# A decoder layer on one core: a new stage order in the attention groups, and FFN preparation moved into the last of them

## What is computed

```python
x = x + attn_ref(layernorm(x), ...)          # one head, softmax over channels
x = x + xattn_ref(layernorm(x), ctx, ...)    # context-query attention
x = x + ffn_ref(layernorm(x), ...)           # mixture of 8 experts and a shared one
# xattn_ref, c = layernorm(x), q = ctx:
s = (c @ w_c + b_c)[:, :, None] + (q @ w_q + b_q)[:, None, :] + cq
a = softmax(s, axis=2);  c2q = a @ q
b_att = softmax(max(s, axis=2), axis=1);  q2c = b_att @ c
z = concat([c, c2q, c * c2q, c * q2c]) @ W_l.T + b_l
# ffn_ref: sigmoid routing picks 4 of 8 experts by groups, weights cw
y = sum_e cw[e] * (silu(x @ Wg[e]) * (x @ Wu[e])) @ Wd[e] + shared(x)
```

## Time and profile before

| | us |
|---|---|
| runs of the kernel | 728.39, 731.85, 733.77 |
| median | 731.85 |
| time of the profiled execution | 728.91 |
| its span, first to last instruction | 726.7 |
| eight attention groups, to the first transposes of the second block | 440.3 |
| FFN block from there | 286.4 |
| PE busy in the span | 674.6 |

### The profile page before, as it was taken

How to read it: one execution, slowest core, us unless ns; L and a number is a source line. 1 busy time by engine, 2 the same in 40 slices (tenths; PEclk the granted TensorE clock), 3 DMA queues, 4 the chain that set the end, 5 groups by cost and what they waited for, 6 DMA issues and landing times. The chain is left out here.

```text
span 726.7 us, 11807 instructions
## 1 busy us (share of the span) xinstructions
PE 674.6 (93%) x3880; PEld 568.7 (78%) x3880; DVE 488.8 (67%) x1253; ACT 346.7 (48%) x793; POOL 243.0 (33%) x321
## 2 busy tenths in 40 slices
PE   3998989999999999999968887999999999999997
PEld 2867968878788788787857576888888888888886
DVE  5577686776776767867675886766666667676432
ACT  3644755565457455664545625433342523433331
POOL 2134364153252542542540412332322232232222
PEclk9999999999999999999997998999999999999999
DMA  7605034042051250430531009131323223030300
GB/s 209 165 25 169 5 83 138 0 135 85 25 157 37 61 159 0 127 93 25 162 102 29 26 15 321 45 129 56 117 88 116 87 98 104 4 143 30 118 29 30
DMA packets 51773, 64.43 MB, mean 89 GB/s; under 512 B 3912, under 2 KB 49528, under 8 KB 50848
## 3 DMA queue, kind: packets, MB, share of 16 engines
q1 hardware_dynamic: 51744, 64.06, 29.0%
HBM read 56.60 MB, written 7.45 MB: 88 GB/s over the span
## 5 line engine op out<-in xcount | busy, mean ns | idle before, releaser
L1515 POOL TENSOR_TENSOR sg<-sg,cw_wide 128x512 f32<-128x512 f32 x56 | 74.6, 1333 | 178.0 <-ACT sg L1476 176.1
L1480 ACT ACTIVATE a_hi<-af 128x512 fp32r<-128x512 f32 x63 | 39.8, 632 | 144.5 <-DVE af L1537 144.5
L1537 DVE TENSOR_TENSOR af<-bank,sg 128x512 f32<-128x512 f32 x63 | 43.3, 687 | 61.6 <-POOL sg L1515 57.1
L75 PE MATMUL bank<-h_hi,w_lo 128*128 128x512 f32 x168 | 67.4, 401 | 1.6 <-DVE w_lo L1554 0.8
L1542 DVE TENSOR_TENSOR a_lo<-af,a_hi 128x512 fp32r<-128x512 f32 x63 | 47.2, 749 | 31.4 <-ACT a_hi L1480 31.4
L76 PE MATMUL bank<-h_lo,w_hi 128*128 128x512 f32 x168 | 66.1, 394 | 0.0
L77 PE MATMUL bank<-h_hi,w_hi 128*128 128x512 f32 x168 | 66.0, 393 | 0.0
L948 POOL TENSOR_TENSOR wz_lo<-tmp,wz_hi 128x512 fp32r<-128x512 f32 x28 | 36.4, 1310 | 44.7 <-ACT wz_hi L732 44.7
L582 PE MATMUL bank<-ctxtf,ctw 128*112 128x375 f32 x128 | 47.0, 489 | 3.0 <-DVE ctw L1089 3.0
L75 PE MATMUL bank<-wl_hi,op_lo 128*112 128x256 f32 x128 | 39.9, 312 | 9.3 <-DVE op_lo L1073 9.3
L75 PE MATMUL bank<-w_hi,a_lo 128*128 128x256 f32 x168 | 47.4, 282 | 0.0
(11 more groups left out here) (229 smaller groups left out, 2059.4 us busy)
## 6 DMA issues: line engine op xcount, KB each, us to landing
ctxtf<-in_ctx_t SPq DMA_DIRECT2D x32, 375.0 KB
ctxf<-in_ctx SPq DMA_DIRECT2D x32, 375.0 KB
cw_wide<-cw_scratch SPq DMA_DIRECT2D x7, 1536.0 KB, 8.0
xt<-in_x SPq DMA_DIRECT2D x8, 448.0 KB, 9.6
x_scratch<-x2b SPq DMA_DIRECT2D x8, 448.0 KB, 3.3
x2n<-x_scratch SPq DMA_DIRECT2D x7, 512.0 KB, 4.6
cw_wide<-cw_scratch SPq DMA_DIRECT2D x7, 512.0 KB, 4.6
x2t<-x_scratch SPq DMA_DIRECT2D x7, 512.0 KB, 3.9
```

The costliest lines, as they stand in the source:

```text
L75: pe.matmul(dst, a_lo, b_hi, start=first, stop=False, **kw)
L1480: act.activation(a_hi[n % (AHEAD + 1)][:, :], af[(p + n) % 2][:, :], ACT.Copy).then_inc(a_hi_ok, 1)
L1515: pool.tensor_tensor(sg[b][:, :], sg[b][:, :], cw_wide[p][:, ORDER[n], :], ALU.mult).then_inc(sgw_ok, 1)
L1537: dve.tensor_tensor(af[b][:, :], u_bank[b][:, :], sg[b][:, :], ALU.mult).then_inc(af_ok, 1)
```

## The change

What it does, engine by engine:

- **All groups, PE.** Stream 3's `z_c` is split into two halves that are put behind `attention_out(3)` and behind `turn_c(2)`; `probs_proj(3)`, `attention_out(1)` and others move a little; `turn_x(3)` and `z_c2q(1)` go ahead of the wait for `mrow`.
- **All groups, ACT and DVE.** `c_weighted` of streams 0 and 1 moves from DVE to ACT (an Identity with scale and bias). On DVE `x1_moments(3)` goes ahead of `sim_max(0)`, and `x2_sum(i - 1, 1)` goes from there to behind `sim_max(2)`. Two one-column copies are added.
- **All groups, POOL.** `c_lo`, and with it `x2b`, waits until `normalise_h` of the next group is done.
- **Front of group 7.** `load_norm(sp, 0)` goes ahead of the nine weight loads. `normalise3(0)` goes behind `probs_low(1)`; `turn_h3(0)` behind `probs_proj(1)`; the shared expert's split on ACT behind `h3_high`; expert 0's and 1's splits to before `ct_copy(0)`; the gate's split to group 0.
- **Rest of group 7.** The second FFN group's `moments3`, `rstd3`, `normalise3` and `turn_h3`, the silu, product and split of the shared expert, the silu input of expert 0 (`sg[1]`) and `gate_up_early` of expert 1 come in. Experts 2 to 5 are loaded into the context's memory as `c2q_product` frees it, and the routing weights are spread to all partitions there. These are taken out of the second block.

The core of the diff:

```diff
                     if last:
+                        for j in range(STAGED):
+                            sp.wait_ge(c2q_mm, G * i + j + 1)
+                            for half, w in enumerate((wg, wu)):
+                                sp.dma_start(gate_up_weights(w_staged[j])[:, half, :, :],
+                                             w[DONE + j].rearrange("(k p) n -> p k n", p=P)).then_inc(wx_in[DONE + j], 16)
+                            sp.dma_start(w_staged[j][:, GU:GU + D], wd[DONE + j]).then_inc(wx_in[DONE + j], 16)
                         sp.wait_ge(cwt_ok, 1)
                         sp.wait_ge(w_in, 16)
                         sp.dma_start(cw_dram[0], cwt[:, :]).then_inc(cw_st, 16)
+                        sp.wait_ge(cw_st, 16)
+                        sp.dma_start(cw_wide0[:, 0:EARLY, :], cw_dram[0][0:EARLY, :].partition_broadcast(P)).then_inc(cw_in, 16)
+                        sp.dma_start(cw_wide0[:, EARLY:NEXP, :], cw_dram[0][EARLY:NEXP, :].partition_broadcast(P)).then_inc(cw_rest_in, 16)
...
+                sp.wait_ge(x2_st, 16 * 3)
+                load_norm(sp, 0)
...
-                sp.wait_ge(x2_st, 16 * 3)
-                load_norm(sp, 0)
                 group(NGRP - 1, True)
...
+                    probs_proj(0)
+                    probs_proj(1)
                     if last_group:
                         pe.wait_ge(v_ok, KB * (i + 1))
                         turn_h3(pe, 0)
-                    probs_proj(0)
-                    probs_proj(1)
                     probs_proj(2)
                     attention_out(0)
+                    probs_proj(3)
+                    attention_out(1)
                     if last_group:
                         pe.wait_ge(gate_ok, 1)
                         logits(pe, 0, h3_hi0, h3_lo0, h_bank[1])
-                    probs_proj(3)
-                    attention_out(1)
                     attention_out(2)
+                    if not is_first(i):
+                        z_c(i - 1, 2)
+                    turn_c(0)
+                    attention_out(3)
                     if last_group:
                         pe.wait_ge(lgt_ok, 1)
                         turn_logits(pe, 0)
                     if not is_first(i):
-                        z_c(i - 1, 2)
-                    turn_c(0)
-                    if not is_first(i):
-                        z_c(i - 1, 3)
-                    attention_out(3)
+                        z_c_half(i - 1, 3, 0)
                     turn_c(1)
                     similarity(0)
                     turn_c(2)
+                    if not is_first(i):
+                        z_c_half(i - 1, 3, 1)
                     similarity(1)
                     turn_c(3)
                     similarity(2)
...
+                    turn_x(3)
+                    z_c2q(1)
                     pe.wait_ge(mrow_ok, i + 1)
-                    turn_x(3)
                     for j in range(G):
                         last = pe.matmul(m_bank[:, j * L:(j + 1) * L], ident[0:G, j:j + 1].to_broadcast([G, P]), mrow[:, :],
                                          start=True, stop=True)
                     last.then_inc(b_mm, 1)
-                    z_c2q(1)
                     z_x3(0)
                     z_c2q(2)
                     z_x3(1)
@@ -706,8 +737,14 @@
                         turn_cw(pe, 0, h_bank[1])
                         pe.wait_ge(w01_lo_ok, 1)
                         gate_up_early(1, wqkv_hi[:, 0, :], wqkv_lo[:, 0, :])
+                        pe.wait_ge(cwt_ok, 1)
+                        pe.wait_ge(cb_ok, i + 1)
+                        turn_h3(pe, 1)
                         for j in range(G):
                             z_c(i, j)
+                        pe.wait_ge(af_ok, 1)
+                        pe.wait_ge(w01_lo_ok, 2)
+                        gate_up_early(0, wqkv_hi[:, 1, :], wqkv_lo[:, 1, :])
...
+                    if last:
+                        h3_high(act, 0, h3_hi0)
+                        act.wait_ge(shared_in, 48)
+                        act.activation(shared_hi[:, 0:GU + D], shared_f[:, :], ACT.Copy).then_inc(shared_hi_ok, 1)
                     probs_proj_copy(2)
                     if last:
+                        act.wait_ge(w01_in, 96)
+                        act.activation(wqkv_hi[:, 0, :], w_f01[:, 0, :], ACT.Copy).then_inc(w01_hi_ok, 1)
+                    probs_proj_copy(3)
+                    if last:
                         copy_logits(act, 0, h_bank[1])
-                    probs_proj_copy(3)
+                        act.activation(wqkv_hi[:, 1, :], w_f01[:, 1, :], ACT.Copy).then_inc(w01_hi_ok, 1)
                     ct_copy(0)
+                    c_weighted(0)
                     ct_copy(1)
+                    c_weighted(1)
...
                     if last:
+                        act.activation(silu_warm[:, :], mhalf2[:, 0:1], ACT.Silu)
+                        act.wait_ge(gu_mm, 1)
+                        act.activation(sg[0][:, :], bank[0][:, :], ACT.Silu).then_inc(sg_ok, 1)
+                        act.wait_ge(af_ok, 1)
+                        act.activation(op_hi0[:, :], af[0][:, :], ACT.Copy).then_inc(a_hi_ok, 1)
+                        copy_cw(act, 0, h_bank[1])
+                        act.wait_ge(gu_mm, 3)
+                        act.activation(sg[1][:, :], bank[1][:, :], ACT.Silu).then_inc(sg_ok, 1)
                         for j in range(G):
                             wz_high(i, j)
-                        copy_cw(act, 0, h_bank[1])
                     else:
                         residual(i + 1)
                         h_high_pair(i + 1, 1)
...
+                    if last:
+                        w01_low(0)
                     for j in range(G):
                         rstd2(j)
-                    if not last:
+                    if last:
+                        rstd3(pool, 1)
+                        w01_low(1)
+                        pool.wait_ge(h3_ok, 2 * T)
+                    else:
                         ln1_scalars(i + 1)
-                    if last:
-                        for e in range(2):
-                            pool.wait_ge(w01_hi_ok, e + 1)
-                            pool.tensor_tensor(wqkv_lo[:, e, :], w_f01[:, e, :], f32(wqkv_hi[:, e, :]), ALU.subtract).then_inc(w01_lo_ok, 1)
+                        pool.wait_ge(hh_ok, G * (i + 2))
                     pool.wait_ge(c_hi_ok, i + 1)
                     pool.tensor_tensor(c_lo[:, :, :, :], ct[:, :, :, :], f32(c_hi[:, :, :, :]), ALU.subtract).then_inc(c_lo_ok, 1)
...
                     c_rows(1)
-                    if last:
-                        dve.wait_ge(wk_in, 48)
-                        sum_logits(dve, 0)
                     dve.wait_ge(st2_ok, ev[2])
-                    c_weighted(0)
+                    dve.tensor_copy(held[0:L, 0:1], mhalf[:, 0:1])
                     x1_moments(2)
                     x1_sum(3)
                     x1_stats(3)
                     c_rows(2)
-                    c_weighted(1)
+                    if last:
+                        dve.wait_ge(wk_in, 48)
+                        sum_logits(dve, 0)
                     dve.wait_ge(st2_ok, ev[3])
+                    dve.tensor_copy(held[0:L, 0:1], mhalf[:, 0:1])
+                    x1_moments(3)
                     sim_max(0)
-                    x1_moments(3)
-                    if not is_first(i):
-                        x2_sum(i - 1, 1)
                     c_rows(3)
                     c_weighted(2)
...
                     for n in range(1, NE):
                         expert(g, p, n)
 
-                with pool.Fori(0, NG2 // 2) as it:
-                    group(2 * it, 0, False)
+                group(0, 0, False)
+                with pool.Fori(0, NG2 // 2 - 1) as it:
                     group(2 * it + 1, 1, False)
+                    group(2 * it + 2, 0, False)
+                group(NG2 - 2, 1, False)
                 group(NG2 - 1, 0, True)
 
             @block.vector
@@ -1554,20 +1616,24 @@
```

154 lines of the change are left out of this document (90 added, 64 removed).

## The result

| | kernel before | changed kernel |
|---|---|---|
| time, median (lowest to highest) | 730.61 us (728.39 to 733.77, 4 runs) | 706.22 us (703.79 to 707.51, 4 runs) |
| ratio to before | | 0.9674, 95% interval 0.9645 to 0.9704 |
| span of the profiled execution | 726.7 us | 703.7 us |

What follows compares the result with a forecast made beforehand. PE, busy 93% of the span, was taken to bound the kernel. 9.0 + 3.5 + 10.5 + 3.5 - 1.0 = 25.5 us saved gives 703.4 us profiled, 706 from the median; 8-in-10 range 697 to 714 us.

Steps and rivals of the forecast that it cites:

- A: Similarity section, all eight groups: PE's stops for c and ctw go, 1.13 us a group, 9.0 us saved.
- B: x_low wait, groups 0 to 6: 1.2 us removed comes back waiting for xt; only clock loss is saved, 3.5 us.
- Rival 4: Similarity section: c still comes from POOL's rstd, the stops stay, A is lost; 715 us, chance 0.04.
- Rival 2: Load of xt doesn't limit; B gives 1.2 us in six more groups; 699 us, chance 0.11.
- The clock recovery: Half-clock losses hidden by the wait for xt go: 2.5 us after group 0, 1.0 after group 2, together 3.5.
- Rival 1: Clock falls at the new stop before probs_proj(0), 1.7 us each, over five groups 8.5; 714 us, chance 0.13.
- C: Front of group 7: x2n lands earlier, first sum comes at 381.7 instead of 392.69; 10.5 us saved.
- D: End of group 7 across the barrier: fourth gate product at 444.6 instead of 448.09; 3.5 us saved, 1.0 lost to clock.
- Rival 5: POOL's held-back work slows x3_low; 1.6 us in each of seven groups reaches PE, 11.5; 717 us, chance 0.04.
- Rival 3: Group 7's new ACT and POOL splits land on the path, taking back C and D's gains; 711 us, chance 0.08.
- Rival 6: Slower: x2_sum(1) slips past c2q_product(0), delaying context loads and xt; at 7 us late, 736 us; chance 0.02.

Runs made afterwards that it cites:

- experiment 2: split_context with c_weighted(0) and (1) back on DVE, 694.61 us; with z_c(3) whole ahead of attention_out(3), 688.71 us; base 686.85 us.
- experiment 1: Changed kernel without POOL's wait for normalise_h, 705.51 us; with context loads split, 686.85; with both edits, 701.12; the split alone on the kernel before, 722.33.
- no_hold: Changed kernel without POOL's wait for normalise_h ahead of c_lo; 705.51 us, ratio 0.9683 to the kernel before.
- norm3_early: split_context with normalise3(0) back ahead of inv_sum(0) in group 7; 688.50 us against the base's 686.85 us.
- experiment 4: Changed kernel with expert 1's gate and up products back behind the barrier, 703.45 us; with split context loads too, 686.57; POOL's expert 1 split also moved, 685.58.
- split_third_w01: Changed kernel with split context loads, expert 1's gate and up products behind the barrier, POOL's low split of expert 1 behind the x2b sums; 685.58 us.
- split_context: Changed kernel with each 125-partition context load cut into 112 and 13 partitions; 686.85 us, ratio 0.9425 to the kernel before.

## Why the prediction was right, and where it wasn't

**The total** was right, 706 forecast and 706.2 measured; 25.5 us were to go, and 24.4 went by the medians (23.0 by the spans). Two terms were off in opposite ways, A 1.4 more than its 9.0 and B 4.1 less than its 3.5, so part of how close the total came is luck.

**A** held. No wait for `ctw` is left, two for `c` are (0.7 us, in group 0), and 8.21 us pass from `turn_c(0)` to `c2q_product(0)` (8.4 forecast). The term was mis-sized by 0.18 us a group; experiment 2 shows that a stop costs two to three times its row. Rival 4 is out.

**B's mechanism** held, and this was the forecast's boldest step: a wait is removed that is the largest sum among PE's in the groups, and nothing is won, since `xt` lands no earlier. `normalise_h` takes 1.37 us (near 1.5), PE waits instead before `probs_proj(0)`, and DVE waits for `xt` by the trace. The four cells of experiment 1 show it as cause, not only as reading. Rival 2 is out: with it the hold would have been worth its price without the split. The clock recovery, "together 3.5", came: after group 0 the gap is 35.15, was 37.80, 2.65 won where 2.5 stood, and after group 2 it is 0.6 shorter, where 1.0 stood. The step that failed is that nothing else moves in B: that `xt` comes as before and that the clock stays up behind the new stop. In group 1 the gap is 39.78, was 36.26, 3.5 us that the sum put at nothing. Rival 1 happened there, once instead of five times: a stop of 3.48 us before `probs_proj(0)`, and 6.8 us at 1.2 GHz behind it. In the other groups the stop was 0.8 to 2.3 us and the clock stayed. The clock is 2.8 us of the 3.5; the other 0.7 I put down to the late load. The stop was that long because `xt` came 26.5 us after `c2q_product(0)`, where the old kernel had 25.0. The changed kernel without the hold (26.3) and the one with the barrier edit (26.3) have it too, the old kernel with the load moved has 24.7; so it belongs to the new order, and not to the hold. In groups 4 to 6 old and new are alike (23.7 to 24.0). What makes it in this one group, I don't know; SP's store of `x2b` goes out 2 us ahead of the first context load in the new order, where it went out 6 us ahead of it, but it does so in all groups.

`no_hold` had no fall of the clock there, with a stop of 1.6 us. Its four runs have mean granted clocks of 0.995 to 0.999, those of the changed kernel 0.989 to 0.995, so it is not a matter of the one profiled execution. But the length of the stop alone doesn't decide: behind the barrier a stop of 2.37 us was followed by 3.4 us at half clock in the changed kernel and by none in `no_hold`.

My size for B, 1.2 us a group, was too small as well: with the load out of the way it is 1.8 (35.3 to 33.5), against rows of 1.16 for `x_low` and, without the hold, a short one for `normalise_h`: again stops that cost more than their rows.

**C** held in size: 10.8 for 10.5. Its first step (the load order moves `x2n` by 3.9) is measured at 3.2 to 3.5. From the statistics of `x2n` to the first sum pass 12.7 us, where 13.0 stood and 20.1 passed before. The rest stands as one chain. The forecast took a normal group's time for it and so, without saying it, a clock at full speed: the 2.8 us at half clock that go here had no term of their own. That `normalise3` in its old place costs 3.5 to 4.5 us, as I expected before `norm3_early` ran, was wrong; it is 1.6.

**D** held: 21.6 us to the fourth gate product (21.3 forecast, 24.8 before), and one stretch of 3.4 us at half clock, 1.5 us lost where I had put 1.0. The 21.6 us have that loss in them, so 3.2 us are won on this stretch for the 2.5 of the sum; 0.8 of it goes again ahead of it, between `c2q_product(0)` and the shared expert's gate product, where the forecast had put nil. The wait for `h3_low` that the sum let stand came as a row of 2.37 us; experiment 4 shows that 0.7 to 1.9 us of it were to be had.

**Rival 5**, POOL over `x3_low`, has the mechanism right and no effect in groups 0 to 6: PE never waits for `x3_low` (L1143) in the changed kernel. Where PE has no cover it bites, as `split_third_w01` shows. **Rival 3**, group 7's new work on the path, came in small: the 0.8 us under D instead of 5. In the trace of `split_context` POOL's split of expert 1 holds a row term of DVE (experiment 4), and PE then waits 1.38 us. **Rival 6** did not come up (its 736 us count six late groups and its 5.6 us count seven; with seven it is 741): the load of `xt` lands as long after `c2q_product(0)` as before, but for the one group above.

## What to carry to other kernels

When two chains meet in each period, compute both lengths before you shorten one. Here they were 35.3 and 35.1 us; the wait on the longer was visible, the other was a load that DVE waited for off PE's path, and each edit alone was worth 0 to 4 us where both were worth 19. Look at the DMA share while a "slow" load runs: a share of a third and SP's issues standing for 3 us were in the profile from the start, and cutting 125 partitions into 112 and 13 brought 19.4 us, where this whole change brought 24.4. And price a stop of PE at more than its row, here by 0.2 to 0.75 us each.

## What the runs showed of the hardware

- Loads of 125 partitions ran at a DMA share of 0.33 to 0.35 and 113 to 117 GB/s while nothing else was on the way. Cut into 112 and 13 partitions, a group's loads ran at 245 GB/s over the whole stretch instead of 167, and took 14.5 us instead of 21.5.
- These DVE operations, whose tensor inputs all lie in SBUF, were held for about the whole of the POOL one beside them: 1.95 us for 0.41 beside 1.81, 4.78 for 1.38 beside 2.56 and 1.84, 2.58 for 1.38 beside 2.56, and 2.14 for 0.37 beside three of POOL's `x2b` sums (3.08 us for four). An operation that reads one of its two inputs from PSUM (`bank`) was not held: 0.37 us beside the last `x2b` sum, in the rows of `split_third_w01`. The Trainium skill (SBUF — State Buffer, SBUF: two separate sides) calls this an exclusive lock, held for the whole instruction, and not a shared rate; here the numbers follow it, and the case of 2.14 us shows that several POOL instructions in a row can hold one DVE instruction.
- Where no load is waited for and the clock doesn't fall, the attention groups become steady: the group period of the kernel with split loads is the same within 0.02 us in groups 1 to 5, and its runs lie within 2.0 us, where those of the changed kernel lie within 3.7.
